# Two-head attention passes: odd heads score in the upper 64 rows, and the product with V moves behind the fourth score

## The reference

```python
q = _split(lora_linear(x, Wq, bq, Bq, Aq))
k = _split(lora_linear(x, Wk, bk, Bk, Ak))
v = _split(lora_linear(x, Wv, bv, Bv, Av))
scores = jnp.einsum('bhqd,bhkd->bhqk', q, k) * SCALE
attn = jax.nn.softmax(scores, axis=-1)
out = jnp.einsum('bhqk,bhkd->bhqd', attn, v)
```

## Time and profile before

| | before |
|---|---|
| median of 3 runs | 353.03 us (352.35 to 353.84) |
| the profiled execution | 353.56 us, of which the span is 351.7 us |
| busy share of the span | PE 92%, DVE 80%, ACT 69%, POOL 37% |
| mean granted TensorE clock | 0.976 |

### The profile page before, as it was taken

How to read it: one execution, slowest core, us unless ns; L and a number is a source line. 1 busy time by engine, 2 the same in 40 slices (tenths; PEclk the granted TensorE clock), 3 DMA queues, 4 the chain that set the end, 5 groups by cost and what they waited for, 6 DMA issues and landing times.

```text
span 351.7 us, 5515 instructions
## 1 busy us (share of the span) xinstructions
PE 324.5 (92%) x1909; PEld 146.1 (42%) x1909; DVE 280.6 (80%) x471; ACT 243.5 (69%) x465; POOL 128.5 (37%) x133
## 2 busy tenths in 40 slices
PE   7999786999979999999999999999998978779796
PEld 3653342222212222222222244338744735447685
DVE  7466999799978999999999543516959997999774
ACT  1575113688858888988888867896479533577694
POOL 5042019999200000000006000400499959995030
PEclk9999998799989999999999999999999989999899
DMA  8937862354340000000000000000000000000011
GB/s 223 315 56 141 140 174 38 64 112 88 64 92 0 1 2 1 2 0 3 0 3 1 1 2 1 2 0 2 0 3 0 1 0 2 0 0 2 1 61 60
DMA packets 14814, 14.57 MB, mean 41 GB/s; under 512 B 4995, under 2 KB 13126, under 8 KB 14598
## 3 DMA queue, kind: packets, MB, share of 16 engines
q1 hardware_dynamic: 12358, 12.09, 15.1%
q10 hardware_dynamic: 2176, 1.64, 1.6%
q0 software_dynamic: 256, 0.52, 0.9%
HBM read 5.78 MB, written 1.05 MB: 19 GB/s over the span
## 4 chain that ended last, share of the span: by engine, by line
PE 63%; SPq 10%; DVE 8%; ACT 7%; POOL 5%; issue 3%; DMA 2%; ACTq 0%; DVEq 0%; POOLq 0%
PE ps L1419 14%; PE ps L1405 12%; SPq L535 8%; PE ps L1559 6%; PE ps L1547 6%; PE ps L1382 5%; PE ps L1334 4%; DVE mx L1097 3%; POOL pbuf L750 3%; PE ps L1532 3%; PE ps L1364 2%; PE ps L1591 2%; DMA pack<-m_rows 1%; ACT ps L931 1%; PE ps L1302 1%
## 5 line engine op out<-in xcount | busy, mean ns | idle before, releaser
L1097 DVE TENSOR_REDUCE mx<-ps 128x1 f32<-128x1024 f32 x128 | 150.3, 1219 | 9.8 <-PE ps L1382 8.6
L888 ACT ACTIVATE pbuf<-ps 128x512 f32<-128x512 f32 x256 | 135.7, 600 | 29.7 <-PE ps L1405 28.6
L1405 PE MATMUL ps<-pack 64*128 64x512 f16 x256 | 87.7, 386 | 3.6 <-DMA pack<-m_rows 1.9
L1419 PE MATMUL ps<-pbuf,v_slot 128*32 128x512 f32 x512 | 69.7, 618 | 1.1 <-ACT parts L873 1.1
L1405 PEld LDWEIGHTS ps<-pack 64*128 64x128 f16 x256 | 23.3, 95 | 82.1 <-ACT pbuf L888 48.5
L1382 PE MATMUL ps<-pack 64*128 64x512 f16 x128 | 49.2, 387 | 5.1 <-DVE mx L1097 4.8
L1382 PE MATMUL ps<-parts,pack 64*128 64x512 f16 x128 | 50.2, 399 | 0.0
L750 POOL TENSOR_TENSOR pbuf<-wT 128x1024 f32<-128x1024 f32 (+3 forms) x32 | 48.2, 1538 | 3.4 <-ACT wT L960 3.4
L705 POOL COPY v_slot<-v_sb 128x512 f32<-128x512 f32 x8 | 4.9, 614 | 113.5 <-PE ps L1419 92.0
L681 POOL TENSOR_TENSOR rstd<-rstd,minus_half 128x2 f32<-128x2 f32 x16 | 11.3, 708 | 71.7 <-DVE rstd L1016 71.7
L1191 DVE SCALAR_TENSOR_TENSOR pack<-ps,g_unit,pack 128x512 f16<-128x512 f32 (+1 forms) x40 | 24.6, 639 | 14.2 <-ACT pack L943 14.1
(11 more groups left out here) (145 smaller groups left out, 392.8 us busy)
## 6 DMA issues: line engine op xcount, KB each, us to landing
w_nat<-in_L_ffn_w_dram SPq DMA_DIRECT2D x2, 1024.0 KB, 6.7
pack<-pack SPq DMA_DIRECT2D x3, 512.0 KB, 4.9
pack<-pbuf SPq DMA_DIRECT2D x20, 64.0 KB, 2.5
x_res<-in_L_attn_a_x_dram SPq DMA_DIRECT2D x4, 256.0 KB, 3.6
pack<-parts SPq DMA_DIRECT2D x16, 64.0 KB, 2.3
pack<-parts SPq DMA_DIRECT2D x32, 32.0 KB, 2.0
out_dram<-x_res SPq DMA_DIRECT2D x4, 256.0 KB, 2.1
w_nat<-in_L_attn_b_Wqkv_dram ACTq DMA_DIRECT2D x1, 768.0 KB, 5.8
```

The source lines that it names most:

```text
L888: act.activation(pbuf[:, c % 2, j, :], ps[:, b, :], ACT.Exp, scale=scale_bits).then_inc(drained[b], 1)
L1097: dve.tensor_reduce(mx[:, par, k:k + 1], ps[:, b:b + 2, :].rearrange("p b k -> p (b k)"), AX_X, ALU.max) \
L1405: pe.matmul(ps[:, b, :], k_group[0:ROWS, at, j, P * c:P * c + P].rearrange("p g t -> p (g t)"), q_rows[0:ROWS, at, qh, j, :].rearrange("p ...
L1419: ins = pe.matmul(ps[32 * j:32 * j + 32, PV_BANK, :], v_slot[:, qh, c, j, :], pbuf[:, c % 2, j, :], start=(c == 0), stop=(c == TT - 1))
```

## The change

Three things are changed together. Keys and queries are now whole in both halves of the array rows, and a score with odd j uses rows 64 to 127 (even j: rows 0 to 63). The product with V of chunk c - 1 stands behind score 4c + 3 and ahead of the max tile that follows that score; the product of a unit's last chunk stands behind score 3 of the next unit, and the shift is turned ahead of score 24 and not 23. Around it: heads 8 to 15 are kept in the same four parts as heads 0 to 7, so a head takes two DMAs and not three or six; group 3 is spread right behind group 2, ahead of the second unit's shift; the shift lands with two DMAs, one per half of the rows; ScalarE waits for groups 2 and 3 before its first copy of `PV_BANK`, whose target shares memory with their parts; and three filler matmuls (`keep_clock`) stand ahead of the last two max tiles of the first unit and ahead of the seven of the lead.

```diff
-SHIFT_AT = 23
+SHIFT_AT = 24
+KEEP_UP = 3
@@ spread
             c, hh = divmod(h, HC)
-            src = slice(HD * hh, HD * hh + HD)
-            if c == 0:
-                eng.dma_start(rows, first_halves[src, m, :, v]).then_inc(done, 16)
-                return
...
+            eng.dma_start(rows, (last_halves if c else first_halves)[HD * hh:HD * hh + HD, m, :, v]).then_inc(done, 16)
@@ sync
-            whole_group(1)
+            spread_group(1)
+            repeat_group(1)
...
-                sp.dma_start(q_rows[SHIFT_ROWS[g // 2], g, qh, :, :].rearrange("o h t -> o (h t)"),
-                             m_rows[0:TWO * n, :]).then_inc(shift_landed, 16)
+                for r in range(TWO):
+                    sp.dma_start(q_rows[slice(ROWS * r + SHIFT_ROWS.start, ROWS * r + SHIFT_ROWS.stop, SHIFT_ROWS.step), g, qh, :, :]
+                                 .rearrange("o h t -> o (h t)"), m_rows[0:TWO * n, :]).then_inc(shift_landed, 16)
...
-            whole_group(2)
+            spread_group(2)
+            spread_group(3)
+            repeat_group(2)
+            repeat_group(3)
...
             land_shift(0, 1, 1)
-            whole_group(3)
             land_shift(1, 0, 2)
@@ scalar
-                src = is_filled(act, ("proj", i)).unsqueeze(1).broadcast_to([P, TWO if c == 0 else 1, HALF])
+                src = is_filled(act, ("proj", i)).unsqueeze(1).broadcast_to([P, TWO, HALF])
...
+                if qh == 0:
+
+                    for n in (2, 3):
+                        act.wait_ge(group_packed[n], GROUP_COUNT)
                 evacuate_pv(g, qh, u)
@@ tensor, score_tile
-                pe.matmul(ps[:, b, :], k_group[0:ROWS, at, j, P * c:P * c + P].rearrange("p g t -> p (g t)"),
-                          q_rows[0:ROWS, at, qh, j, :].rearrange("p g t -> p (g t)"), start=True, stop=True) \
+                rows = slice(ROWS * (j % 2), ROWS * (j % 2) + ROWS)
+                pe.matmul(ps[:, b, :], k_group[rows, at, j, P * c:P * c + P].rearrange("p g t -> p (g t)"),
+                          q_rows[rows, at, qh, j, :].rearrange("p g t -> p (g t)"), start=True, stop=True) \
                     .then_inc(filled[b], 1)
@@ tensor, first and second max passes
+                if k >= FILLS - 2:
+                    pe.wait_ge(drained[PV_BANK], base[PV_BANK])
+                    keep_clock(KEEP_UP, PV_BANK)
                 max_tile(0, 0, 0, k)
...
             for k in range(LEAD):
+                keep_clock(KEEP_UP, PV_BANK)
                 max_tile(0, 1, 1, k)
@@ tensor, unit
                         score_tile(*nxt, s - STEPS)
+                    if s == G - 1 and before is not None:
+                        times_v(*before, TT - 1)
+                    elif s % G == G - 1 and s > G:
+                        times_v(qh, u, s // G - 1)
                     if s % 2 == 1:
                         if fill < FILLS and nxt is not None:
                             max_tile(*nxt, fill)
                         elif fill >= FILLS and after is not None:
                             max_tile(*after, fill - FILLS)
                         fill += 1
-                    if s % G == 2 and s > G:
-                        times_v(qh, u, s // G - 1)
```

More of the change, by code:

```diff
@@ L510, in term, with keys @@
         def term(c, m, which, v):
-            if c == 0:
-                return first_halves[:, m, (0, 1 if m == K_ else 2, 3)[which], v]
-            return last_halves[:, m, which, v]
+            return (last_halves if c else first_halves)[:, m, (0, 1 if m == K_ else 2, 3)[which], v]
         def first_terms(c, m, v):
-            if c == 0:
-                return first_halves[:, m, 0:3:2, v] if m == K_ else first_halves[:, m, 0:2, v]
-            return last_halves[:, m, 0:1, v]
+            halves = last_halves if c else first_halves
+            return halves[:, m, 0:3:2, v] if m == K_ else halves[:, m, 0:2, v]
         def spread(eng, rows, m, h, v, done):
             c, hh = divmod(h, HC)
-            src = slice(HD * hh, HD * hh + HD)
-            if c == 0:
-                eng.dma_start(rows, first_halves[src, m, :, v]).then_inc(done, 16)
-                return
[L529 to L541, removed]
+            eng.dma_start(rows, (last_halves if c else first_halves)[HD * hh:HD * hh + HD, m, :, v]).then_inc(done, 16)
+        def keys(eng, h, r, v, done):
+            spread(eng, k_rows[ROWS * r:ROWS * r + ROWS, h, v], K_, h, v, done)
         def queries(eng, h, r, qh, done):
@@ L602, in _, with spread_group, repeat_group @@
             for j in range(G):
[L603 removed]
+                keys(sp, j, j % 2, second_half if j % 2 == 0 else first_half, score_keys_packed)
             sp.wait_ge(second_half_packed, 16 * G)
             sp.dma_start(q_rows[ROWS:2 * ROWS, 0, 1, :, :], q_rows[0:ROWS, 0, 1, :, :]).then_inc(second_half_repeated, 16)
[L607 removed]
+            def spread_group(g):
                 for h in range(G * g, G * g + G):
[L609 to L614, removed]
+                    keys(sp, h, 0, whole, group_packed[g])
+                    both_queries(sp, h, group_packed[g])
+            def repeat_group(g):
+                sp.wait_ge(group_packed[g], GROUP_COUNT)
+                sp.dma_start(k_rows[ROWS:2 * ROWS, G * g:G * g + G, :].rearrange("p h t -> p (h t)"),
+                             k_rows[0:ROWS, G * g:G * g + G, :].rearrange("p h t -> p (h t)")).then_inc(group_repeated[g], 16)
                 sp.dma_start(q_rows[ROWS:2 * ROWS, g, :, :, :].rearrange("p s j t -> p (s j t)"),
                              q_rows[0:ROWS, g, :, :, :].rearrange("p s j t -> p (s j t)")).then_inc(group_repeated[g], 16)
[L618 removed]
+            spread_group(1)
+            repeat_group(1)
             def land_shift(g, qh, u):
@@ L906, in _ @@
                 act.wait_ge(head_packed_by_pool[j], 32)
-            for done in (far_keys_packed, second_half_packed):
+            for done in (score_keys_packed, second_half_packed):
                 act.wait_ge(done, 16 * G)
-            act.wait_ge(group_packed[1], group_count(1))
+            act.wait_ge(group_packed[1], GROUP_COUNT)
             for s in range(G):
@@ L1379, in max_tile @@
                     pe.wait_ge(drained[b], base[b] + u * (FILLS // 2) + k // 2)
-                for n, keys in ((0, k_group[0:ROWS, at, j, 0:HALF]), (1, far_group[ROWS:2 * ROWS, at, j, :])):
-                    q = q_rows[ROWS * n:ROWS * n + ROWS, at, qh, j, P * qt:P * qt + P]
-                    ins = pe.matmul(ps[:, b + n, :], q.rearrange("p g t -> p (g t)"), keys.rearrange("p g t -> p (g t)"),
+                for n in (0, 1):
+                    rows = slice(ROWS * n, ROWS * n + ROWS)
+                    ins = pe.matmul(ps[:, b + n, :], q_rows[rows, at, qh, j, P * qt:P * qt + P].rearrange("p g t -> p (g t)"),
+                                    k_group[rows, at, j, HALF * n:HALF * n + HALF].rearrange("p g t -> p (g t)"),
                                     start=True, stop=True)
@@ L1448, in _, with unit @@
             pe.wait_ge(pads, 1)
-            pe.wait_ge(group_packed[1], group_count(1))
+            pe.wait_ge(group_packed[1], GROUP_COUNT)
             pe.wait_ge(group_repeated[1], 32)
-            def unit(g, qh, u, nxt, after):
+            def unit(g, qh, u, nxt, after, before):
                 fill = LEAD
```

41 lines of the change are left out of this document (20 added, 21 removed).

## The result

The changed kernel takes 366.52 us (median of 4 runs, 365.14 to 367.95), the one before 353.05: a ratio of 1.040 (95% interval 1.035 to 1.044), 13.5 us slower. I forecast 357.7. The profiled execution took 365.14 us, its span is 363.3 us, its mean granted clock 0.986. TensorE is now busy 88% of the span, VectorE 77%, ScalarE 67%.

A forecast was written before the change was run, and what follows sets the result against it. The round trip of one bank, 2.39 us per chunk, was taken as the bound; +11.2 - 0.9 - 1.6 - 3.4 + 0.3 - 0.7 - 0.2 = +4.7 on 353.0 gave 357.7 us, range 354.8 to 363.

The forecast's parts named there:

- the round trip: Exp pass: exp, score, product, next score and its exp follow around one bank and set the chunk's period, 2.39 us.
- The chunk, +11.2: Exp pass, units 0 to 6: max tile between product and score lengthens a chunk from 2.39 to 2.61; 51 x 0.22 us.
- The second shift, +0.3: SP's queue: four repeats of 512 KB now ahead of the second shift; up to 1 us late, +0.3 taken.
- The start, -0.7: Up to exp 8 of unit 0: fillers keep the clock up, that exp at 65.3 instead of 66.05; bounds +1.3 and -2.
- The third shift, -3.4: SP's queue: nothing stands ahead of the third shift any more, so its score does not wait; -3.4 us.
- The copy of the sum, -1.6: Unit ends: the next unit's first product no longer waits for the copy, 0.26 us each, six times; -1.6.
- The shift, -0.9: Each turned shift between product and score costs about 0.2 us instead of 0.33, seven times; -0.9.
- The last unit, 0: Last unit: its list is unchanged and full of 128-row work, so upper rows give nothing there.
- The -0.2 for the last product of unit 6: End of unit 6: last product stands as before, with a smaller distance to its score; -0.2 us.
- that pairing pays: Rival: the round trip does not bind and scores side by side save time; 346.5 or 339.5 us, chance 0.14.
- The falling clock: Rival, exp pass: TensorE's idling lowers its clock, 1.34 us per slow chunk; 371 for ten, 362 for three; chance 0.07.

The follow-up runs named there:

- e6: Changed kernel with two waits of ScalarE exchanged, so head 0's exp waits for room in `pbuf` first and for its score last: 365.57 us, ratio 1.037.
- e3: Changed kernel with the second unit's shift landed ahead of group 3's repeats and the two bias loads in SP's queue: 363.54 us, ratio 1.029.
- e7: Kernel before with one DMA moved: third shift issued behind group 3's 24 DMAs but ahead of their wait and repeats: 350.48 us, ratio 0.991.
- e4: Changed kernel with all scores in the lower rows again, group 0's second keys spread there to match: 369.61 us, ratio 1.047.
- e10: e8 with all scores, odd heads' too, in the lower rows of TensorE: 352.46 us, ratio 0.999.
- e1: Changed kernel with the product with V back behind score 4c + 2 and the shift ahead of score 23: 356.15 us, ratio 1.008.
- e8: Changed kernel with e1's and e3's edits, product back ahead of score 4c + 3 and second shift ahead of group 3's repeats: 350.04 us, ratio 0.992.

## Why the prediction was right in kind and wrong in size

The direction and its cause held: the round trip binds, a max tile between product and score is added in full, and it falls to 2.39 without max tiles. The size failed in two terms of the sum, the second shift and the last leg of the chunk, and both made the kernel slower than forecast. The steps, with what each measured against exp 8 of unit 0 and exp 0 of unit 7:

- **The chunk, +11.2.** The legs were right but the last. I took 0.42 from score to exp, read from the exp of head 3, which has no wait for `pbuf`; the new late score is head 0's. With 0.50 the chunk is 2.69 in units 0 to 5, and a unit takes 21.8 to 21.9 us and not 21.1: 46 x 0.30 + 5 x 0.22 = 14.9. Mis-sized by 3.7. e6 shows that the 0.08 is ScalarE's.
- **The second shift, +0.3.** This step failed most. "It may be up to 1 us late" has no price for issuing the four repeats, and does not name the two bias loads that stand behind them. From the first repeat to the shift the queue took 10.2 us (72.07 to 82.29), where in the kernel before two repeats and the same two loads took 4.2 (74.09 to 78.27): SP stood 1.3 waiting for group 3's spreads to land, and the last repeat and the two loads took over 2 us of issue each, where before the first of these loads took 0.69. It cost +5.1 beyond chunks of 2.69: 3.4 of waiting beyond the usual 0.62, the rest in the slow chunks behind it. Undone in e3.
- **The start, -0.7.** It was +0.6. Up to the first exp the changed kernel is 2.0 behind (59.55 against 57.57), and from there to exp 8 it takes 7.1 us and not 8.5. The delay is made of the last two max tiles of unit 0, which wait for `drained[PV_BANK]` and then for fillers (VectorE idles 1.29 there), and of the first shift's second DMA. I had called that DMA hidden, which holds for seven shifts but not for the first: its score waits for it at once, 3.3 us from issue to exp against 2.6.
- **The third shift, -3.4:** no wait is left. With the 0.2 by which the last chunk of unit 0, which needs the second shift, was over 2.39 before, -3.6. e7 shows the same gain alone.
- **The copy of the sum, -1.6:** chunks with it take 2.67 in units 3 and 5 and 2.77 in units 2 and 4, against 2.69, so it is all but free and -1.4. **The shift, -0.9:** it still costs 0.27 a time where I took 0.2, so -0.5.
- **The last unit, 0:** -1.8, by the upper rows (e4, e10). The argument "full of 128-row work, so upper rows give nothing" was wrong: a pair makes its 128-row neighbour start 0.21 earlier. The -0.2 for the last product of unit 6 lies in the same stretch and can't be told from it.

Again with these sizes: 14.9 + 5.1 - 3.6 - 1.4 - 0.5 + 0.6 - 1.8 = 13.3; the marks of the trace gave 13.2, and the median rose by 13.5. Of the rivals, that pairing pays was refuted by e1, e4 and e10 for units 0 to 6. The falling clock, which the prediction counted as a sign of being wrong, came in unit 1 behind the second shift's stall and not from the chunks: from 133.5 to 155.5 us it is 1.00.

## What to carry to other kernels

Follow a round trip to its last leg with the very instruction that will stand there: the same exp starts 0.08 us later when another instruction takes the wait for its score, and that times fifty is more than many a change. When DMAs are moved ahead of a small urgent one in the same queue, take the price of their issue from a place where as much is queued ahead of them, and put the urgent one first. Work that runs side by side pays where the engine's own work is the limit, as in the last unit; in a round trip that closes over another engine the time gained is waited away.

## What the hardware showed that I had not expected

- How long SP takes to issue a DMA depends, as far as these runs tell, on what is queued ahead of it more than on its size. Of the four repeats of 512 KB the first three took 0.60, 0.83 and 0.66 us and the fourth 2.31, and the bias loads of 128 KB behind it 2.27 and 2.06. In e8 the third and the fourth took 0.54 and 0.60, and the loads behind them 2.54 and 1.78. The share of busy DMA engines alone doesn't tell when: it is 0.96 from 72.07 to 74.80, over the first two, and 0.99 from there to the shift. The sixteen spreads of 128 KB took 0.88 on the mean, each between 0.60 and 1.36. The Trainium skill (Perfetto Trace Analysis, DMA Instruction — HWDGE (DVE, Sync)) says that the window the profiler reports covers making the descriptors, and not the movement of the data; so this is time in which the queue is closed to the shift; the trace agrees, since each of the last four issues, from 75.51 on, begins 0.04 to 0.06 us after the end of the one before.
- A score's exp starts 0.41 us after the score if the exp itself waits for the score, 0.47 to 0.48 if a semaphore instruction ahead of it does, and 0.50 if a register instruction does.
